# A recommender tower (CIN and MLP) on one core: ids first, chunk 0's copies on two queues, layer 1's first group in halves, the sums over d apart and the table rows' splits one group later

## The reference, cut to what matters

```python
z0 = einsum('bid,bjd->bdij', x0, x0);  cur0 = relu(einsum('bdk,kl->bld', z0, W0))     # 1521 products
next_h, direct0 = split(cur0, 2, axis=1)                                              # 64 and 64
z1 = einsum('bid,bjd->bdij', x0, next_h);  cur1 = relu(einsum('bdk,kl->bld', z1, W1)) # 2496 products
z  = sum(concatenate([direct0, cur1], axis=1), axis=-1)                               # sums over d
h  = relu(concatenate([z, dense_ctx]) @ W_top1 + b_top1); h = relu(h @ W_top2 + b_top2)
y  = h @ W_top3
```

## Time and profile before

| | us |
|---|---|
| three runs | 444.56, 441.90, 439.06 (median 441.9) |
| the profiled execution | 437.52, its span 435.7 |
| busy in the span | PE 400.6, DVE 345.7, POOL 294.6, ACT 226.0 |
| mean granted clock of TensorE | 0.978 |
| chain that ended last, by share | POOL 44%, PE 39%, issue 9% |

### The profile page before, as it was taken

The page is one execution under the profiler, slowest core; times in us unless marked ns, Lnnn a source line. Parts: engine busy times, 40 slices in busy tenths (PEclk is TensorE's granted clock), DMA queues, the critical chain, the costliest instruction groups (busy, mean ns, idle before and its releaser), DMA issues.

```text
span 435.7 us, 4074 instructions
## 1 busy us (share of the span) xinstructions
PE 400.6 (92%) x1426; PEld 249.0 (57%) x1426; DVE 345.7 (79%) x196; ACT 226.0 (52%) x224; POOL 294.6 (68%) x164
## 2 busy tenths in 40 slices
PE   0868977999999899999999799999999999997897
PEld 0734634666666546666656356565656565664464
DVE  0305748799999798999998788999999989999800
ACT  3025544474738356564746273847475656553422
POOL 3778889888888888888888888898989800000000
PEclk9989998999999989999999799999999999999999
DMA  8384956496969497878879493959886888992000
GB/s 309 81 218 128 260 135 176 123 247 187 242 165 265 120 262 178 232 199 216 210 214 222 138 281 78 290 137 233 195 253 187 219 218 226 261 253 56 2 0 0
DMA packets 27862, 80.80 MB, mean 185 GB/s; under 512 B 7265, under 2 KB 16225, under 8 KB 20034
## 3 DMA queue, kind: packets, MB, share of 16 engines
q1 hardware_dynamic: 22146, 77.64, 65.9%
q0 software_dynamic: 5120, 1.32, 3.3%
q10 hardware_dynamic: 576, 1.58, 1.1%
HBM read 76.58 MB, written 3.93 MB: 185 GB/s over the span
## 4 chain that ended last, share of the span: by engine, by line
POOL 44%; PE 39%; issue 9%; DMA 3%; DVE 3%; ACT 0%; DVEq 0%
POOL found L277 44%; PE acc L499 7%; PE acc L531 6%; PE acc L524 5%; PE acc L523 5%; PE acc L542 5%; PE sums L482 3%; DMA found<-in_table_dram,rows_sb 2%; PE acc L538 2%; DVE z_lo L418 2%; PE spread L571 2%; DMA ids_sb<-in_ids_dram 1%; PE spread L512 1%; DVE z L410 1%; PE sums L560 1%
## 5 line engine op out<-in xcount | busy, mean ns | idle before, releaser
L277 POOL DMA_INDIRECT found<-in_table_dram,rows_sb x160 | 294.4, 1840 | 53.6 <-issue 48.5
L320 ACT ACTIVATE z_hi<-z 128x2048 fp32r<-128x2048 f32 x64 | 122.4, 1912 | 95.5 <-DVE z L410 95.5
L418 DVE TENSOR_TENSOR z_lo<-z,z_hi 128x2048 fp32r<-128x2048 f32 x64 | 145.8, 2279 | 0.0
L410 DVE TENSOR_TENSOR z<-x_wide,h 128x2048 f32<-128x2048 f32 x64 | 144.8, 2281 | 0.0
L499 PE MATMUL acc<-squares,w 128*128 128x512 f32 (+1 forms) x224 | 110.8, 612 | 0.0
L523 PE MATMUL acc<-z_hi,w_hi 128*128 128x512 f32 x256 | 107.3, 419 | 0.7 <-ACT cur L313 0.7
L524 PE MATMUL acc<-z_hi,w_lo 128*128 128x512 f32 x256 | 101.0, 394 | 0.0
L531 PE MATMUL acc<-z_lo,w_hi 128*128 128x512 f32 x256 | 84.3, 452 | 10.7 <-DVE z_lo L418 10.7
L296 ACT ACTIVATE squares<-sums 128x1024 f32<-128x1024 f32 x64 | 58.4, 913 | 35.5 <-PE sums L482 35.5
L531 PEld LDWEIGHTS acc<-z_lo,w_hi 128*128 128x128 f32 x256 | 47.9, 190 | 36.4 <-issue 15.2
L499 PEld LDWEIGHTS acc<-squares,w 128*128 128x128 f32 (+1 forms) x224 | 41.8, 192 | 28.8 <-issue 24.6
(11 more groups left out here) (44 smaller groups left out, 134.0 us busy)
## 6 DMA issues: line engine op xcount, KB each, us to landing
x_wide<-x_rows SPq DMA_DIRECT2D x64, 512.0 KB, 8.1
x_wide<-x_rows SPq DMA_DIRECT2D x112, 256.0 KB, 9.9
x_parts<-x_rows SPq DMA_DIRECT2D x32, 128.0 KB, 2.6
x_rows<-found SPq DMA_DIRECT2D x16, 240.0 KB, 2.2
x_wide<-x_rows SPq DMA_DIRECT2D x16, 192.0 KB, 7.2
found<-in_table_dram,rows_sb POOLq DMA_INDIRECT x160, 7.6
w_sb<-in_w_dram SPq DMA_DIRECT2D x1, 1280.0 KB, 8.1
x_wide<-x_rows SPq DMA_DIRECT2D x16, 64.0 KB, 6.7
```

Of the source, the lines that this page charges most:

```text
L277: pool.indirect_dma_start(out=found[:, b, 2, s * D:s * D + D], out_offset=None, in_=table, in_offset=bass.IndirectOffsetOnAxis(ap=rows_sb[ ...
L320: nc.scalar.activation(z_hi[:, n % RING], z[:, n % RING], ACT.Copy).then_inc(hi_done, 1)
L410: nc.vector.tensor_tensor(z[:, n % RING], x, h[:, c % 2, :].unsqueeze(1).to_broadcast([P, QUADS, N]), ALU.mult).then_inc(multiplied, 1)
L418: nc.vector.tensor_tensor(z_lo[:, n % RING], z[:, n % RING], z_hi[:, n % RING], ALU.subtract).then_inc(lo_done, 1)
```

## The change

It does the following, all in the order of the work and its semaphores; no arithmetic is added or left out.

1. ACT issues its four loads of weights only when `ids_in` has come; before, they were issued at once. DVE computes chunk 0's row numbers in an instruction of their own (10 columns), then the other 150; POOL waits for each.
2. Chunk 0's two `place` DMAs are issued by SP and by ACT, one each; before, both by SP.
3. Chunk 0's group 0 is multiplied in two halves by DVE, rounded in two halves by ACT, and PE starts on the first half.
4. DVE's two sums over d no longer stand together: `reduce0(c + 1)` comes behind the low part at g = 4, `reduce1(c - 1)` behind the low part at g = 1. The splits from chunk 3 on move from g = 0 to g = 1, on ACT and on DVE.
5. On ACT, squares stand ahead of `evict1` at g = 0 in the first chunks, and `evict0` of chunk 1 comes one group earlier. `keep_busy` ahead of the first sums has 36 matmuls in place of 30.

```diff
--- before.py
+++ after.py
@@ block.sync @@
-            def place(c):
-
-                b = c % BUFS
-                sp.wait_ge(rows_out[b], 16 * uses(c))
-                for half in range(2):
...
-                place(c)
+                place(sp, c, 0)
+
+                if c:
+                    place(sp, c, 1)
@@ block.gpsimd @@
-            pool.wait_ge(rows_ready, 1)
             for c in range(CHUNKS):
                 b = c % BUFS
+                if c < 2:
+                    pool.wait_ge(rows_ready, c + 1)
@@ block.scalar @@
+            act.wait_ge(ids_in, 16)
             act.dma_start(select_in, select).then_inc(select_in_done, 16)
...
             split(0)
+            place(act, 0, 1)
             for d in range(ND):
                 square(d)
             split(1)
             evict0(0)
-            high_part(0)
+            act.wait_ge(half_multiplied, 1)
+            nc.scalar.activation(z_hi[:, 0, 0:2], z[:, 0, 0:2], ACT.Copy).then_inc(half_hi_done, 1)
+            act.wait_ge(multiplied, 1)
+            nc.scalar.activation(z_hi[:, 0, 2:], z[:, 0, 2:], ACT.Copy).then_inc(hi_done, 1)
...
-                    if g == (2 if c else 3) and c + 1 < CHUNKS:
+                    if g == 2 and c + 1 < CHUNKS:
                         evict0(c + 1)
-                    if n == 2:
-                        split(2)
-                    if g == 0 and 0 < c < CHUNKS - 2:
+                    if g == 1 and c + 2 < CHUNKS:
                         split(c + 2)
@@ block.vector @@
-                    if n == 3:
-                        split(2)
                     if n + 1 < G * CHUNKS:
                         multiply(n + 1)
-                    if g == G - 1 and c + 1 < CHUNKS:
-
-                        reduce0(c + 1)
-                        if c:
-                            reduce1(c - 1)
+                    if n == 2:
+                        split(2)
                     if is_v(n):
                         low_part(n)
                     if n == 0:
                         reduce0(0)
-                    if g == 0 and 0 < c < CHUNKS - 2:
+                    if g == 1 and 0 < c < CHUNKS - 2:
                         split(c + 2)
-                    if n == G * (CHUNKS - 1) + 1:
-                        reduce1(CHUNKS - 2)
+                    if g == 1 and c:
+                        reduce1(c - 1)
+                    if g == G - 1 and c + 1 < CHUNKS:
+                        reduce0(c + 1)
@@ block.tensor @@
-            keep_busy(acc0, 30)
+            keep_busy(acc0, 36)
```

More of the change, by code:

```diff
@@ L170, in build @@
         multiplied = sem("multiplied")
+        half_multiplied = sem("half_multiplied")
         hi_done = sem("hi_done")
+        half_hi_done = sem("half_hi_done")
         lo_done = sem("lo_done")
@@ L187, in uses, with place @@
             return c // BUFS + 1
+        def place(queue, c, half):
+            b = c % BUFS
+            queue.wait_ge(rows_out[b], 16 * uses(c))
+            start = x_rows[b, half, 0, 0:1]
+            queue.dma_start(x_parts[half:P:2, b, :].bitcast(F32),
+                            bass.AP(start.tensor, start.offset, [[N, 2 * STEP], [STEP * N, QUADS], [1, N]])
+                            ).then_inc(placed[b], 16)
         block = ctx.enter_context(nc.Block())
@@ L353, in _ @@
                     n = G * c + g
+                    if g == 0 and c < 2:
+                        square(ND * (c + 1))
                     if g == 0 and c:
                         evict1(c - 1)
-                    if g == 0 and c < 2:
-                        square(ND * (c + 1))
                     if n == 0:
@@ L433, in _ @@
             dve.wait_ge(ids_in, 16)
-            nc.vector.tensor_tensor(rows_sb[:, :, :], ids_sb[:, 1:, :],
-                                    ids_sb[:, 0:1, :].to_broadcast([P, CHUNKS, SLOTS]), ALU.add).then_inc(rows_ready, 1)
+            nc.vector.tensor_tensor(rows_sb[:, 0, :], ids_sb[:, 1, :], ids_sb[:, 0, :], ALU.add).then_inc(rows_ready, 1)
+            nc.vector.tensor_tensor(rows_sb[:, 1:, :], ids_sb[:, 2:, :],
+                                    ids_sb[:, 0:1, :].to_broadcast([P, CHUNKS - 1, SLOTS]),
+                                    ALU.add).then_inc(rows_ready, 1)
             dve.wait_ge(w0_in, 32)
@@ L448, in _ @@
             split(1)
-            multiply(0)
+            dve.wait_ge(h_ready, 2)
+            dve.wait_ge(spread_done, 1)
+            nc.vector.tensor_tensor(z[:, 0, 0:2], spread[:, 0:2, :],
+                                    h[:, 0, :].unsqueeze(1).to_broadcast([P, 2, N]), ALU.mult).then_inc(half_multiplied, 1)
+            nc.vector.tensor_tensor(z[:, 0, 2:], spread[:, 2:, :],
+                                    h[:, 0, :].unsqueeze(1).to_broadcast([P, 2, N]), ALU.mult).then_inc(multiplied, 1)
             for c in range(CHUNKS):
@@ L519, in contract1_hi @@
                     pe.wait_ge(evicted1, c)
-                pe.wait_ge(hi_done, v_count(n))
+                pe.wait_ge(*((hi_done, v_count(n)) if n else (half_hi_done, 1)))
                 for a in range(QUADS):
                     t = slot1(g) + a
+                    if n == 0 and a == 2:
+                        pe.wait_ge(hi_done, 1)
                     nc.tensor.matmul(acc1[:, :], w1_hi[:, t, :], z_hi[:, r, a, :], start=(t == 0), stop=False)
```

## The result

The changed kernel takes **460.8 us** (median of four runs, 459.47 to 463.43), the kernel before 442.0 (439.06 to 444.56): 1.044 times the time, 95% interval 1.036 to 1.052. It is slower. The profiled execution took 460.9 us, with a span of 459.1 where it was 435.7.

The account below looks back on a forecast made before the run. PE was taken to bound a good chunk at 22.25 us, with stalls from late gathers. From the profiled 437.5: 437.5 - 1.2 + 50 - 9.8 = 476.5, predicted as 478 us; range 462 to 500, over both signs 423 to 500.

Parts of the forecast that it names:

- What bounds it: PE bounds a good chunk at 22.25 us; DVE's stops for late table rows add 9.8 us in all.
- The hold behind a lone reduction: At `z(1)` behind `reduce0`, a gather starting 0.6 us into the product is held to the reduction at 14.45 us.
- the layout: DVE's operations in one chunk at PE's pace, from PSUM's product on: 5 gathers start where 10 are needed.
- The hold behind split and `reduce1`: At `z(3)`, a gather starting at 15.65 us is held to DVE's pause at 21.65, unless the split was waited for.
- The length of a chunk: Ten gathers set it: 28.3 us, or 25.8 with one hold place; 26.4 taken, 4.15 over the floor in 12 chunks.
- the old stops: DVE's stops ahead of splits in two pairs of chunks, 3.70 and 6.10 us; their 9.8 us come off.
- The start: Ids landing sooner and a shorter first add let POOL start earlier: -1.2 us, the middle of 0 to 2.5.
- that stop covers them: DVE's 7.31 us stop at chunk 0 for chunk 2's gathers hides the microsecond or two its first products move.
- What would show it: Signs in the profile after: gathers over 8 us, DVE idle ahead of splits, PE waiting for z_lo, chunks of 26 to 28 us.
- The gathers keep up: Rival, chance 0.34: every shut-out gather passes at the next operation's end, ten fit into 22.25 us; 426.5 or 431 us.
- The hold ends with the third operation: Rival, chance 0.07: the gather behind `z(1)` is freed at `z_lo(1)`; a chunk of 23.6 us, +16 us, 443 us.
- The late spread: Rival, chance 0.03: x_wide's spread exceeds its 1.0 us to spare in some chunks, costing PE 10 us: 437 us.

Follow-up runs that it names:

- drained: The changed kernel plus a wait on DVE for `reduce0` ahead of the product that follows it: 448.7 us, beside 477.4 for the changed kernel in that batch.
- r0_ahead: The changed kernel with `reduce0` alone moved right ahead of the product from PSUM: 448.4 us, beside 480.3 for the changed kernel in that batch.
- splits_again: The changed kernel with both reductions back behind the product from PSUM, splits still in group 1: 456.4 us, beside 461.9 for the kernel before.
- sums_only: The changed kernel with the splits from chunk 3 on back in group 0, sums apart: 465.8 us, 1.024 of the kernel before.

## Why the prediction was right, and where it was off

The forecast was the likeliest case, slower by holds: 478 us, 462 to 500 on its own. Measured: 460.8, just under its lower end and inside the range over both signs. By its steps:

- **What bounds it.** Right. At each stop PE waits at the end of the line gathers, ACT's split, DVE's split, copy.
- **The hold behind a lone reduction.** Right in the place that decides. The row at 243.46 is the one that the layout put 0.6 us behind `z(1)`. There was luck in it: by the rule that I had, any reduction would do, and the one ahead of `z(1)` happened to be `reduce0`.
- **The hold behind split and `reduce1`.** None in the profile after. I had given the pattern as any reduction without a pause behind it. The trace of before could not clear `reduce1`: in nine of its 11 held rows both stood together, in two (at 46.05 and 67.78) `reduce0` stood alone, and in none `reduce1`. It was `reduce0`, and the forecast reached `z(3)` only in rows that no split interrupts.
- **The length of a chunk: mis-sized.** Taken 26.4 us in 12 chunks, +50; measured 41.5 us over the floor in 14, a mean of 25.2. With one place alone the layout gave 25.8. About half of the holds ended at a pause ahead of `z_lo(1)` (6.9 us, not 9.1), which my layout did not have: from split to split their chunks took 24.7 us in the mean, those with 9.1 us 25.6. The hold's length is not all: the last such chunk, with 4.7 us, took 27.3.
- **Less the old stops,** 9.8 us: measured 10.3.
- **The start: mis-sized,** -1.2 taken, -7.8 measured. POOL's first gather came at 3.35 us, 0.15 outside the bounds (3.5 to 5.5) that I had named as the sign of a wrong start, and 2.2 us earlier, not 1.2. What failed is "that stop covers them": I took the 7.31 us at chunk 0 as a fixed stop that an earlier start only shortens by its own size. It hung on one gather, the tenth of chunk 2, being held. With POOL 2.2 us earlier it got out ahead of the hold. This, 6.6 us, the chunks' 8.5 (50 less 41.5) and 0.5 of the old stops are the 15.6 us between the sum of 476.5 and the profiled 460.9.
- **The start on PE's side.** DVE's first product began at 38.31 where it was 38.24, so queues and halves gained PE nothing.
- **What would show it.** Gathers over 8 us behind `z(1)`: in six chunks, 6.9 or 4.7 in seven others. DVE idle ahead of the split by 4 to 7 us: 2.5 to 5.3. A chunk of 26 to 28: 23.3 to 27.3 from chunk 1 to chunk 13, then 22.3 and 23.5. PE waiting for z_lo: wrong; 1.0 us in all, against 31.2 for `x_parts`.
- **The rivals.** *The gathers keep up* fell, and it is what `drained` and `r0_ahead` restore. The Trainium skill, page "SBUF — State Buffer", section "SBUF: two separate sides", has the lock of the shared port pair held for one whole instruction. The 135 gathers with `reduce1` alone in their row and those of `drained` agree, but end 0.9 us behind the next start and not 0.115; the hold of 9.09 us over four instructions does not, and the measurement decides. *The hold ends with the third operation* fell at 243.46, held over four. *The late spread* did not show: where chunks kept PE's pace (`splits_again`) they took 22.26 us.

## What to carry to other kernels

When an engine's queue of small gathers feeds a pipeline, look at the longest gathers, not at the mean, and at every operation that the other engine issued since it last paused: one instruction far back in an unbroken row can decide. Ask which item of a batch a stall hits; one place earlier or later in the order moved a split by 5 us. A wait of a tenth of a microsecond in the right place was worth over twenty here.

## What the runs showed of the hardware

- Behind a reduction over 64 partitions (64x512 to 64x32, `reduce0`), up to DVE's next pause, POOL's indirect DMA did not get in between operations with two SBUF inputs, with one exception: 89 gathers of 4.7 to 18.4 us. Behind the reduction over 128 partitions (128x512 to 128x32) it got in, in 135 cases of 135. A pause of 0.1 us, put in on purpose, cleared it; so did pauses from 0.03 us up that came by themselves. Whether the 64 partitions, the source or the target make the difference was not tried.
- In the experiments' profiles ACT stood for up to 18 us (in `sums_only` once for 41) with no wait that the trace names, while POOL made gathers 1.25 us apart. One wait on POOL took 20 us off a median of 453.5 and 7 off the lowest time.
- The same kernel before took 442 us in its first runs and 455 to 462 on the chips of the three batches; in the experiments' profiles of those chips chunk 0's product starts at 65 to 89 us instead of 54.
